# Image rotation on TensorE: two further matmuls per step, whose result nobody reads

## The reference

```python
x = x + attn(cond(x, subject))            # 16 heads, causal
x = x + local_ffn(rigid_transform(x, fside, angle))   # rotation, then 6 layers
x = x + gla(diffusion(x, zX, zY, zR))
x = x + moe(typed_experts(x))
```

## Time and profile before

| | before |
|---|---|
| median of three runs | 2743.41 us |
| lowest, highest | 2739.4, 2743.43 us |
| the profiled execution | 2736.72 us |
| its span, first to last instruction | 2734.9 us |
| mean granted TensorE clock over the span | 0.973 |
| TensorE matmuls busy | 2519.4 us, 92% |
| VectorE busy | 2095.3 us, 77% |
| ScalarE busy | 1899.0 us, 69% |
| GpSimd busy | 1778.8 us, 65% |

### The profile page before, as it was taken

The page is one execution under the profiler, slowest core; times in us unless marked ns, Lnnn a source line. Parts: engine busy times, 40 slices in busy tenths (PEclk is TensorE's granted clock), DMA queues, the critical chain, the costliest instruction groups (busy, mean ns, idle before and its releaser), DMA issues.

```text
span 2734.9 us, 98096 instructions
## 1 busy us (share of the span) xinstructions
PE 2519.4 (92%) x36165; PEld 1721.1 (63%) x36169; DVE 2095.3 (77%) x4531; ACT 1899.0 (69%) x6651; POOL 1778.8 (65%) x1605
## 2 busy tenths in 40 slices
PE   6989888888999999999999999999999999879999
PEld 4656544445666666666666666666666666648884
DVE  6777677767888888888888888888888888765644
ACT  3666666656878787878877888888888878633323
POOL 1666765544977787877787788778777777521210
PEclk8999989988999999999999999999999999989999
DMA  4000010002111211111111211121112111100000
GB/s 134 11 11 10 12 45 10 10 9 69 35 32 32 56 39 38 33 49 45 41 32 36 58 41 32 32 62 40 33 32 62 37 36 32 43 1 1 1 1 16
DMA packets 177425, 92.28 MB, mean 34 GB/s; under 512 B 40950, under 2 KB 173257, under 8 KB 176977
## 3 DMA queue, kind: packets, MB, share of 16 engines
q1 hardware_dynamic: 168352, 82.00, 11.7%
q0 software_dynamic: 8192, 4.21, 1.1%
q10 hardware_dynamic: 432, 0.07, 0.0%
HBM read 32.06 MB, written 3.76 MB: 13 GB/s over the span
## 4 chain that ended last, share of the span: by engine, by line
POOL 35%; PE 20%; issue 11%; DVE 7%; ACT 3%; DVEq 0%; POOLq 0%; SPq 0%; DMA 0%; ACTq 0%
POOL rs L1507 17%; POOL t_pair L1497 12%; POOL pr L1488 5%; PE bank L1115 2%; PE scores L1160 1%; PE bank L1171 1%; PE bank L1108 1%; PE bank L1799 1%; PE bank L1823 1%; PE bank L1200 1%; PE scores L1142 1%; ACT pr L1430 1%; PE bank L2056 1%; PE bank L1793 1%; DVE qr_pair L1342 1%
## 5 line engine op out<-in xcount | busy, mean ns | idle before, releaser
L1507 POOL TENSOR_TENSOR rs<-ssc,neg_half 128x8 f32<-128x8 f32 x384 | 648.5, 1689 | 32.6 <-DVE ssc L1378 32.6
L1497 POOL TENSOR_TENSOR t_pair<-qn_pair,tabs 128x512 f32<-128x512 f32 x384 | 489.2, 1274 | 13.3 <-DVE qn_pair L1362 11.0
L1430 ACT ACTIVATE pr<-scores,negmax 128x64 f32<-128x64 f32 x1536 | 463.5, 319 | 4.3 <-DVE negmax L1387 0.4
L1488 POOL TENSOR_TENSOR pr<-pr,rec 128x256 f32<-128x256 f32 x384 | 235.7, 614 | 329.7 <-DVE rec L1355 329.7
L1108 PE MATMUL bank<-wqk,xs 128*128 128x512 f32 x768 | 396.1, 598 | 4.8 <-DVE qn_pair L1362 3.6
L1011 POOL DMA_INDIRECT rg_win<-rg_images,share_down x256 | 255.2, 997 | 139.9 <-DVE rg_prod L950 84.4
L1424 ACT COPY vt<-bank 128x256 f32<-128x256 f32 x361 | 134.6, 373 | 278.0 <-PE bank L1171 240.5
L1430 ACT ACTIVATION_READ_ACCUMULATOR pr<-scores,negmax 128x1 f32 x1536 | 321.7, 209 | 0.0
L1115 PEld LDWEIGHTS bank<-ident,qr_pair 128*128 128x128 f32 x1536 | 180.0, 142 | 183.1 <-DVE qr_pair L1342 145.9
L1362 DVE TENSOR_TENSOR qn_pair<-bank,rs 128x512 f32<-128x512 f32 x384 | 260.6, 679 | 23.1 <-POOL rs L1507 22.7
L1342 DVE TENSOR_TENSOR qr_pair<-t_pair 128x512 f32<-128x512 f32 x384 | 264.9, 690 | 10.7 <-issue 0.7
(11 more groups left out here) (309 smaller groups left out, 5609.7 us busy)
## 6 DMA issues: line engine op xcount, KB each, us to landing
rg_prod<-vt SPq DMA_DIRECT2D x1536, 32.0 KB
wqk<-in_L_ffn_Wqkv SPq DMA_DIRECT2D x20, 256.0 KB
rg_win<-rg_images,share_down POOLq DMA_INDIRECT x256
wv<-in_L_ffn_Wqkv SPq DMA_DIRECT2D x20, 128.0 KB
wo<-in_L_ffn_Wo SPq DMA_DIRECT2D x20, 128.0 KB
w<-in_L_ffn_W SPq DMA_DIRECT2D x6, 341.0 KB
rg_images<-rg_prod SPq DMA_DIRECT2D x1, 1625.0 KB, 7.7
rg_images<-XT SPq DMA_DIRECT2D x16, 64.0 KB
```

The source lines that it names most:

```text
L1430: ex = act.activation(pr[t % 2][:, h * BAND:(h + 1) * BAND], sl_ps[:, h // 2, h % 2 * BAND:(h % 2 + 1) * BAND], ACT.Exp, bias=negmax[t % 2 ...
L1488: pool.tensor_tensor(p, p, over(rec[t % 2][:, :], [P, GH, BAND], 2), ALU.mult).then_inc(a.p_scaled, 1)
L1497: pool.tensor_tensor(t2[t % 2][:, :].rearrange("p (i h f e) -> p i h f e", i=2, h=GH, f=2), qn[t % 2][:, :].rearrange("p (i h f e) -> p i ...
L1507: pool.tensor_tensor(rs[t % 2][:, :], ssc[t % 2][:, :], neg_half[:, 0:8], ALU.pow)\
```

## The change

After each `cut(k)`, TensorE issues two more matmuls. Their weights are 32 columns of `rg_place`, one takes rows 0 to 63 of the array and the other rows 64 to 127, their moving data are the first 256 columns of `XT` (512 in the first five steps, which have no placement), and they write partitions 0 to 31 and 32 to 63 of the first bank of `scores`. No semaphore is waited for or raised, and nothing reads the result. Nothing else is changed.

```diff
+            def occupy(size):
+
+                for two in range(2):
+                    rows_ = slice(two * HALF, (two + 1) * HALF)
+                    pe.matmul(scores[two * WIN:(two + 1) * WIN, 0, 0:size], rg_place[rows_, 0:WIN], XT[rows_, 0:size],
+                              start=True, stop=True, skip_group_check=True)
             for k in range(B * RG_STEPS + RG_LATE):
                 if k < B * RG_STEPS:
                     cut(k)
+                    occupy(2 * P if k >= RG_LATE else CW)
                 if k >= RG_LATE:
                     place(k - RG_LATE)
```

## The result

The kernel with the pair took 2750.34 us (median of 15, 2741.08 to 2759.47), the kernel before, measured again beside it, 2741.53 (median of 15, 2728.64 to 2748.48). The ratio is 1.0034, with a 95% interval of 1.0019 to 1.0049: 9 us slower, where 13 us faster was forecast. The time lies in the range that was given, but on the wrong side of no change.

The account below looks back on a forecast made before the run. The prediction took TensorE to bound the image stage, starved while gathers run, its clock falling behind thin stretches. Its terms, 13 + 0 - 26 = -13 us, took 2743.4 us to 2730 us, range 2706 to 2760.

Parts of the forecast that it names:

- What bounds the stage: Image stage, 307 us: TensorE is what others wait for, starved in thin stretches while gathers run, the clock falling behind them.
- Term 1, the pair's work: TensorE, all 64 steps: the pair takes 0.48 us warm, 0.2 us a step counted, 13 us added; between 0 and 33.
- Term 2, the switch of shape: Tile shape between cut and placement: no switch added in 59 steps, two each in the first five; counted as nothing.
- Term 3, the clock: TensorE's clock in the image stage: the pair avoids falls and so cold time, 26 us gained; between 0 and 40.
- fewer than six pieces: Sign in the profile after: the stage has fewer than six pieces at clock 0.50, its granted clock 0.93 or more.
- the falls that have an added pair in the thin stretch before them go: Image stage: clock falls with a pair in the thin stretch ahead vanish, above all in the first steps; 26 us gained.
- the first rival: Image stage: the pair comes too late behind the cuts, the falls stay, 20 us slower, 2763 us; chance 0.28.
- The dampening of the cycle: Image stage: steps of 3.4 us instead of 2.9 space the gathers and weaken the loop of clock and thin stretches.
- It cancels: Image stage: 10 to 15 us of cold time go and the added work costs the same, 2743 us; chance 0.15.
- The work is free: Image stage: idle time takes the pair up and the clock never falls, 35 us gained, 2708 us; chance 0.12.
- if the clock rises and the stage isn't shorter, the pair's price was taken too low: Sign in the profile after: a higher granted clock without a shorter image stage means the pair's cost was underestimated.

Follow-up runs that it names:

- s4_mid_cut: The change with the pair moved between the two halves of the cut and left out of the first five steps: ratio 1.0064 to the kernel before (2729.67 us).
- r2: The change, unchanged, run again beside the kernel before (2740.23 us) on a chip with thin stretches: ratio 1.0028.
- s2: The change, unchanged, run again in a later series beside the kernel before (2729.67 us): ratio 1.0065.
- r1: The kernel before, unchanged, profiled again on a chip with thin stretches, where before took 2740.23 us: ratio 0.9994.
- s1: The kernel before, unchanged, profiled again in a later series, where before took 2729.67 us: ratio 0.9998.

## Why the prediction was wrong, point by point

*What bounds the stage.* Right for the chips of the first profiles, and confirmed: thin stretches, the clock falling behind them, gathers as a condition. What it could not see from one profile is that all this belongs to some chips; the same kernel takes 236 us for the stage on two chips of those used, and 292 to 309 on the others where a profile of before was taken.

*Term 1, the pair's work.* 0.48 us a step was read for the work and 0.42 measured (3.28 - 2.86). What of it is on the path in a warm step was taken as 0.2 and measured as 0.27 to 0.33 in the three pairs of profiles: 16 to 19 us over 59 steps instead of 12. In the first five steps it is 2.4 to 4.2 us. The term is mis-sized by about a half: 13 us forecast, some 20 by this reckoning, an estimate that lets cold steps pay as warm ones do, which no run shows by itself.

*Term 2, the switch of shape.* Counted as nothing. In s4_mid_cut, which adds two switches, a step without gathers is 10.7 / 3 = 3.57 us against the 3.30 of the change, so 0.27 for a pair with its two switches more; TensorE is busy without a break in it (4.00 of the 4 us from 640). The pair in the placement's shape avoids that in 59 steps. In the first five steps each pair adds two switches, 5 x 0.27 = 1.4 us by this number, an estimate that lies within the 2.4 to 4.2 above. The Trainium skill, TensorEngine Tiling (Array Packing), section Tiling Modes, says that a change of mode drains the engine. The 0.27 us fit that, though no row shows the drain by itself.

*Term 3, the clock: the step that failed.* The forecast let the pair prevent more than half of the cold time, and took 26 us, with "fewer than six pieces" as the test. There are 13 in the change's profile as before, 12 in r2 and s2 as in r1 and s1, 11 with twice the work. Where the thin stretch lies in the cuts, 3 to 4 us long, the pair waits behind them in the order of the list. Where it lies in the placements, the pair has run ahead of it, and the clock falls all the same (554.9); and in the first steps the thin stretch is in the pair itself (360.4). So the step "the falls that have an added pair in the thin stretch before them go" failed, and with it its reason, that placements keep the clock up even when thin. What changed was on the other side of the fall: nine of 13 pieces last 3.4 us instead of two. That the pair's work behind the cold cuts is the cause is argued from the order of the list and not tested by itself; the series of s1 has no less cold time with the pair (65 us against 61). The 24 us less cold time were worth some 11 us (20 - 9, a remainder and not a measurement), where 26 were forecast. Of the 22 us between -13 and +9, this term has some 15 and term 1 some 7. The Trainium skill's rule in TensorE: Matmul & The Clock Gate, section HAM oscillation — how this bites in real kernels, which lays the falls to pauses of the engine, was weighed beside the first rival and was the better guide here: the pauses stayed, and so did the falls, 13 before and 13 after.

*The dampening of the cycle* by a slower step was an argument without a row. The period of twelve steps is there after as before, in the same place.

*The rivals.* The first, "the falls stay", had 0.28 and named the mechanism, with 20 us as its price. Measured are 8 to 15; on two of the three chips the cold pieces got shorter, which that rival had not in its sum. "It cancels" describes the middle on the two chips of r1 and of the first profiles. "The work is free" came true on two chips, for another reason than the one given: VectorE is the bound there, and there is no fall to prevent. The sign "if the clock rises and the stage isn't shorter, the pair's price was taken too low" came, with 0.91 instead of the 0.93 or more of the forecast, and names the smaller part of the miss.

## What to carry to other kernels

Filler work in an engine's list did not hold its clock through pauses that hold up the list itself, whether it stood ahead of the pause, amid it or behind it; look at what causes the pause, since the filler costs its part on the path and at best shortens the recovery. Before pricing an effect of feeding or of memory, take the profile of the unchanged kernel on more than one chip: here its times differ by 2.7%, and the change costs 0.0 to 0.65%. And price work added in steps without idle time (first and last ones) by itself.

## What the runs showed of the hardware that was not expected

The unchanged kernel took 2670.5, 2672.0, 2727.3, 2729.7, 2730.8, 2740.2 and 2741.5 us in the seven series, two of these (2740.2 and 2727.3) on the same chip in different series. By the profiles the whole difference is in the image stage: span less stage is 2741.5 - 308.8 = 2432.7 in r1_before, 2721.2 - 292.4 = 2428.8 in s1_before, and 2670.9 - 236.3 = 2434.6 for the change on the last chip. On the slower ones, matmuls and their weight loads come one to five at a time, 0.7 us apart, while gathers run. The traces speak against the nearest reasons. These are the queues of the gathers (software_dynamic) and of the instructions in the first 238 us of the stage, kernel before, and the change on the last chip (packets, MB, share of the 16 DMA engines):

```profile
q0 software_dynamic: 3776, 1.94, 5.6%
q8 instruction: 23, 0.38, 0.7%
```

```profile
q0 software_dynamic: 4512, 2.32, 8.1%
q8 instruction: 35, 0.57, 1.0%
```

Worked out from these lines, an instruction transfer takes about 1.2 us in the first and 1.1 in the second, and a packet of a gather 56 and 68 ns. Neither is markedly slower where the stretches are thin; there are only fewer of them in the same time. So slow transfers, of windows or of instructions, don't explain the thin stretches. What does hold TensorE up while gathers run, and what differs between the chips, no run shows.
